# Row sums that are inverted later: raw heads and raw sums leave the attention, and a batched reciprocal and a scaling follow before the output projection

## The reference

```
qkv = x @ w_qkv.T + b_qkv                      # 16 heads of 32
scores = q @ k.T / sqrt(32) + causal mask
attn = softmax(scores); out = attn @ v
x = layernorm(x + out @ w_out.T + b_out)
hidden = relu((x @ sign(up_w).T) * up_scale)   # 2048 wide
x = layernorm(x + (hidden @ sign(down_w).T) * down_scale * output_scale)
```

## Time and profile before

| | us |
|---|---|
| median of 3 runs | 765.48 (764.55 to 766.41) |
| the profiled execution's own time | 763.71 |
| its span in the trace | 761.9 |
| PE busy | 720.6 (95%) |
| DVE busy | 439.5 (58%) |

### The profile page before, as it was taken

How to read it: one execution, slowest core, us unless ns; L and a number is a source line. 1 busy time by engine, 2 the same in 40 slices (tenths; PEclk the granted TensorE clock), 3 DMA queues, 4 the chain that set the end, 5 groups by cost and what they waited for, 6 DMA issues and landing times.

```text
span 761.9 us, 11587 instructions
## 1 busy us (share of the span) xinstructions
PE 720.6 (95%) x4032; PEld 504.0 (66%) x4032; DVE 439.5 (58%) x990; ACT 317.5 (42%) x631; POOL 353.5 (46%) x487
## 2 busy tenths in 40 slices
PE   6899999999999999999989889999999999999993
PEld 4688665665656656565544545887878787878882
DVE  4276495785967859578467652443393349325515
ACT  5211365555656546565456575333222222222210
POOL 4461467394673946739422503632352235223333
PEclk9999999999999999999989999999999999999998
DMA  6976455535555355453577333221012001000101
GB/s 234 310 202 176 107 149 149 144 112 154 150 146 140 109 160 146 124 144 96 154 235 249 103 120 113 69 103 63 1 42 98 28 1 55 3 1 15 41 1 55
DMA packets 44618, 85.70 MB, mean 112 GB/s; under 512 B 4880, under 2 KB 13584, under 8 KB 44432
## 3 DMA queue, kind: packets, MB, share of 16 engines
q1 hardware_dynamic: 35536, 79.72, 34.4%
q10 hardware_dynamic: 9024, 5.24, 2.4%
HBM read 55.33 MB, written 29.36 MB: 111 GB/s over the span
## 4 chain that ended last, share of the span: by engine, by line
PE 74%; DVE 14%; DMA 4%; issue 3%; POOL 2%; ACT 2%; SPq 0%; ACTq 0%; POOLq 0%
PE ps_heads L1039 9%; PE ps_proj L941 8%; PE ps_proj L1081 7%; PE ps_score L1098 6%; PE ps_unit L1081 6%; PE ps_unit L1057 6%; PE ps_sum L1033 5%; PE ps_unit L977 4%; DVE maxes L811 4%; PE ps_unit L1009 4%; DVE heads_sb L830 4%; PE ps_heads L1098 3%; PE ps_sum L1098 3%; PE ps_score L1009 3%; PE ps_score L977 2%
## 5 line engine op out<-in xcount | busy, mean ns | idle before, releaser
L653 POOL TENSOR_TENSOR hid_low<-hid_raw,hid_high 128x512 fp32r<-128x512 f32 x64 | 85.0, 1328 | 174.4 <-DVE hid_high L880 171.3
L709 ACT ACTIVATE probs<-ps_unit 128x512 f32<-128x512 f32 (+3 forms) x216 | 101.9, 490 | 82.6 <-PE ps_unit L1009 80.7
L617 POOL TENSOR_SCALAR_AFFINE_SELECT probs<-probs 128x128 f32<-128x128 f32 x256 | 72.6, 297 | 105.1 <-ACT probs L709 100.6
L709 ACT ACTIVATE probs<-ps_score 128x512 f32<-128x512 f32 (+3 forms) x155 | 75.2, 498 | 74.4 <-PE ps_score L1009 73.0
L880 DVE CAST hid_high<-hid_raw 128x512 fp32r<-128x512 f32 x64 | 27.1, 424 | 125.5 <-ACT hid_raw L764 125.2
L807 DVE CUSTOM_DVE_ANT_0 ps_unit<-ps_unit,causal 128x512 f32<-128x512 f32 (+3 forms) x162 | 80.0, 511 | 32.4 <-PE ps_unit L977 31.8
L977 PE MATMUL ps_unit<-stack 96*128 96x512 f32 (+3 forms) x246 | 83.7, 353 | 5.4 <-DVE maxes L807 2.5
L1039 PE MATMUL ps_heads<-probs,v_rows 128*32 128x512 f32 (+3 forms) x768 | 79.5, 497 | 4.1 <-DVE heads_sb L832 4.1
L1009 PE MATMUL ps_unit<-stack 98*128 98x512 f32 (+2 forms) x216 | 78.7, 367 | 3.3 <-DVE maxes L807 3.2
L611 POOL TENSOR_TENSOR parts<-qk_full,parts 128x512 fp32r<-128x512 f32 x32 | 41.2, 1287 | 64.1 <-ACT parts L688 64.1
L811 DVE TENSOR_REDUCE maxes<-ps_unit 128x1 f32<-128x512 f32 x84 | 55.0, 682 | 19.0 <-PE ps_unit L977 18.9
(11 more groups left out here) (195 smaller groups left out, 1439.3 us busy)
## 6 DMA issues: line engine op xcount, KB each, us to landing
stack<-qk_parts SPq DMA_DIRECT2D x96, 256.0 KB, 4.5
qk_parts<-parts SPq DMA_DIRECT2D x32, 512.0 KB, 3.0
v_all<-h_even ACTq DMA_DIRECT2D x16, 256.0 KB, 3.8
v_rows<-v_all SPq DMA_DIRECT2D x8, 512.0 KB, 4.4
heads_t<-heads_sb SPq DMA_DIRECT2D x16, 256.0 KB, 3.4
raw<-up_w SPq DMA_DIRECT2D x8, 512.0 KB, 4.2
x_tile<-x_rows SPq DMA_DIRECT2D x16, 256.0 KB, 5.1
raw<-down_w SPq DMA_DIRECT2D x8, 512.0 KB, 3.5
```

Source lines behind the costliest of these rows:

```text
L653: nc.gpsimd.tensor_tensor(hid[1][:, (HM * s + n) % 3, :], hid_raw[:, n % 2, :], hid[0][:, (HM * s + n) % 3, :].bitcast(FP32), ALU.subtract ...
L709: nc.scalar.activation(probs[:, (NP * s + n) % RING, 0:width], bank(what, s, n)[:, off:off + width], ACT.Exp, scale=SCALE).then_inc(s_exp, 1)
```

## The change

The job `norm` becomes `copy`: DVE copies `ps_heads` to `heads_sb` and `ps_sum` to a new `sums_sb`, and SP stores both; of the sums it stores one row for each of the 4 heads. All sums of a batch of steps are then loaded as one tile of 128 partitions (`gather`), inverted by DVE (`invert`, L904 in the new file), stored (`scatter`), and spread with a broadcast over 32 partitions into the buffer that later takes the high parts (`spread`, four DMAs of 256 KB for each chunk). A new DVE job `scale` multiplies the loaded heads by it (L909), before ACT and DVE split them. There are four batches: steps 0 to 5; step 6's first half; its second half; step 7. PE's wait before L1039 is now for the copied heads only, and one before L1033 for the copied sums. The table `MAXIMA` is spaced more evenly in its first two thirds.

```
-PAIRED_NORM = [19.73, 52.08]
+PAIRED_COPY = [19.73, 52.08]
-MAXIMA = ([11.5 + 0.5 * u for u in range(3)] + [13.4 + 0.48 * u for u in range(13)]
-          + [26.3 + 0.6 * u for u in range(3)] + [28.4 + 0.53 * u for u in range(14)] + [37.5 + 0.66 * u for u in range(15)])
+MAXIMA = ([11.5 + 0.7 * u for u in range(16)] + [23.4 + 0.73 * u for u in range(17)] + [37.5 + 0.66 * u for u in range(15)])
+BATCHES = [(0, STEPS - 2, 0, 2), (STEPS - 2, STEPS - 1, 0, 1), (STEPS - 2, STEPS - 1, 1, 2), (STEPS - 1, STEPS, 0, 2)]
+COLUMNS = [0, 192, 208, 224, 256]
...
-            put(t + at, "norm", s, q)
-            put(t + at + 4.9, "store", s, q)
+            put(t + at, "copy", s, q)
+            put(t + at + 1.6, "store", s, q)
...
+    for k, at in enumerate((late + 8.5, late + 22.5, last + 6.5, FIRST_UP + 2)):
+        put(at, "gather", k)
+        put(at + (2.9 if k < 3 else 1), "invert", k)
+        put(at + (4.4 if k < 3 else 1.5), "scatter", k)
+    put(late + 28.6, "spread", 0)
+    put(last + 14, "spread", 1)
...
+        put(late + 37 + 2 * i, "scale", 0, i)
         put(late + 38 + 2 * i, "split", 0, i)
+        put(last + 30 + 2 * i, "scale", 1, i)
...
                 put(t - 4, "fetch", i + 1)
+                put(t + 0.2, "spread", i + 1)
...
+                if i:
+                    put(t + 1.7 + 0.7 * q, "scale", i + 1, q)
                 put(t + 2.2 + 0.7 * q, "split", i + 1, q)
...
+                if what == "gather":
+                    _, end, _, f1 = BATCHES[s]
+                    sp.wait_ge(s_sst[0], 16 * end)
+                    sp.wait_ge(s_sst[1], 16 * (end if f1 == 2 else end - 1))
+                    sp.dma_start(columns(s), batch(sums_dram, s)).then_inc(s_gat, 16)
+                if what == "scatter":
+                    sp.wait_ge(s_inv, s + 1)
+                    sp.dma_start(batch(inv_dram, s), columns(s)).then_inc(s_sca, 16)
+                if what == "spread":
+                    f, b = s % 2, s // 2
+                    sp.wait_ge(s_sca, 16 * (2, 3, 4, 4)[s])
...
+                    for h in range(GH):
+                        sp.dma_start(inverses(s)[h * HD:(h + 1) * HD, :, :],
+                                     inv_dram.rearrange("(g b f h q) -> g b f h q", b=2, f=2, h=GH, q=HALF)[:, b, f, h, :]
+                                     .partition_broadcast(HD)).then_inc(s_spr, 16)
...
                 if what == "split":
+                    act.wait_ge(s_nrm, DC * s + n + 1)
...
-                    nc.vector.reciprocal(heads_sb[:, :], ps_sum[:, :]).then_inc(s_rc, 1)
-                    dve.wait_ge(s_rc, 2 * s + n + 1)
-                    nc.vector.tensor_tensor(heads_sb[:, :], ps_heads[:, :], heads_sb[:, :], ALU.mult).then_inc(s_norm, 1)
+                    nc.vector.tensor_copy(heads_sb[:, :], ps_heads[:, :]).then_inc(s_hc, 1)
+                    wait(dve, s_sst[1 - f], 16 * (s + f))
+                    nc.vector.tensor_copy(sums_sb[:, :], ps_sum[:, :]).then_inc(s_norm, 1)
+                if what == "invert":
+                    dve.wait_ge(s_gat, 16 * (s + 1))
+                    nc.vector.reciprocal(columns(s), columns(s)).then_inc(s_inv, 1)
+                if what == "scale":
+                    if n == 0:
+                        dve.wait_ge(s_hl, 16 * (s + 1))
+                        dve.wait_ge(s_spr, 16 * GH * (s + 1))
+                    nc.vector.tensor_tensor(heads_in(s)[:, n, :], heads_in(s)[:, n, :], inverses(s)[:, n, :],
+                                            ALU.mult).then_inc(s_nrm, 1)
```

More of the change, by code:

```diff
@@ L152, in plan @@
             put(t + 43.9, "sum_added", s)
-        for q, at in enumerate(PAIRED_NORM if paired else ALONE_NORM[s % 2]):
-            put(t + at, "norm", s, q)
-            put(t + at + 4.9, "store", s, q)
+        for q, at in enumerate(PAIRED_COPY if paired else ALONE_COPY[s % 2]):
+            put(t + at, "copy", s, q)
+            put(t + at + 1.6, "store", s, q)
         if s + 1 < STEPS:
@@ L262, in build @@
         heads_dram = nc.dram_tensor("heads_t", [GROUPS, P, TOKENS], FP32, kind="Internal").ap()
+        sums_dram = nc.dram_tensor("sums", [STEPS * 2 * GH * HALF], FP32, kind="Internal").ap()
+        inv_dram = nc.dram_tensor("inverses", [STEPS * 2 * GH * HALF], FP32, kind="Internal").ap()
         qk_dram = nc.dram_tensor("qk_parts", [2, NB, P, 2, HALF], FP32, kind="Internal").ap()
@@ L298, in build @@
         s_pv = sem("probs_used")
-        s_rc = sem("row_sum_inverted")
+        s_hc = sem("heads_copied")
+        s_sst = [sem(f"sums_stored{f}") for f in range(2)]
+        s_gat = sem("sums_gathered")
+        s_inv = sem("sums_inverted")
+        s_sca = sem("inverses_stored")
+        s_spr = sem("inverses_spread")
+        s_nrm = sem("heads_scaled")
         s_add = sem("probs_added")
         s_used = sem("added_probs_used")
-        s_norm = sem("heads_normalized")
+        s_norm = sem("heads_and_sums_copied")
         s_st = [sem(f"heads_stored{f}") for f in range(2)]
@@ L346, in build @@
         rstd2 = sb(top, "rstd2", [P, 2], FP32)
+        inv = sb(top, "inv", [P, COLUMNS[-1]], FP32)
         h1_even = sb(top, "h1_even", [P, TT, D], FP32)
@@ L427, in heads_in, with inverses, columns, batch @@
             return heads_raw if s else h1_even
+        def inverses(s):
+            return turned[s % 2][0][:, :, :].bitcast(FP32)
+        def columns(k):
+            return inv[:, COLUMNS[k]:COLUMNS[k + 1]]
+        def batch(dram, k):
+            s0, s1, f0, f1 = BATCHES[k]
+            return dram[(2 * s0 + f0) * GH * HALF:(2 * s1 - 2 + f1) * GH * HALF].rearrange("(p c) -> p c", p=P)
         def bank(what, s, n):
@@ L724, in _ @@
                     else:
+                        if n == 15:
+                            for f in range(2):
+                                act.wait_ge(s_sst[f], 16 * STEPS)
                         if n == 16:
@@ L1022, in _ @@
                     if what == "pv" and j == 0:
-                        wait(pe, s_norm, 2 * s + f)
+                        wait(pe, s_hc, 2 * s + f)
                         if f == 0:
                             pe.wait_ge(s_vl[s % 2], 16 * (s // 2 + 1))
+                    if what == "sum" and j == 0:
+                        wait(pe, s_norm, 2 * s + f)
                     for h in range(GH):
```

19 lines of the change are left out of this document (14 added, 5 removed).

## The result

The changed kernel is slower: 769.50 us median against 764.07 of the kernel before on the same chip, a ratio of 1.0075 (95% interval 1.0057 to 1.0092). In a second session, unchanged (label after_again), it took 767.67 against 763.98, 1.0049 (1.0030 to 1.0068). The profiled execution took 767.28 us with a span of 765.5; before it was 763.71 and 761.9.

The account below looks back on a forecast made before the run. PE was taken to set the time, DVE counting only where PE waits. Terms -10 + 0 + 2.4 - 2.3 + 11.2 = +1.3 us on 763.7 gave 765.0, median 766.8; range 762 to 770 (chance 0.50).

Parts of the forecast that it names:

- Steps 0 to 5: Attention steps: gain of 10 us, 3.6 from heads waits and 6.4 from row maxima; bounds 3.6 and 13.
- signs that the prediction named: Inversion and PE waits with clock 0.50 in step 6; 3.5 us projection waits, clock below 1; no `heads_sb` waits; step 45.5 us.
- Middle of step 6: Reciprocal's 5.7 us stall goes, about 5.7 returns as DVE waits for gathered sums: 0; bounds gain 5.5, loss 2.
- End of step 6: Four `scale` products on DVE, which paces PE there, cost 2.4 us; bounds 0 and 4.5.
- Step 7: Waits for `heads_sb` (0.81 us) and h_even (1.42 us) go: gain of 2.3 us, bounds 0.8 and 4.
- Feed-forward part: PE waits 3.4 us more at each of two chunks, clock falls cost 2.2 each: loss of 11.2 us.
- (2): Rival: POOL stretches the scaling, each chunk waits up to 7.3 us: slower, 776.6 us; chance 0.21 (above 770).
- (1): Rival: gain stays, clock holds in feed-forward and gather lands within 2.2 us: 757.6 us; chance 0.29 together with (3).
- (3): Rival: nothing felt, attention not DVE's and scaling covered, only step 6's 5.7 us goes: 759.8; chance 0.29 with (1).

Follow-up runs that it names:

- e7: Kernel before with its reciprocal of the row sums replaced by a copy, so the division is left out; 765.49 us, ratio 1.0016.
- e6: Changed kernel with the old table MAXIMA of the kernel before; 776.57 us, ratio 1.0157 to the kernel before.
- e5: Kernel before, division as it was, with only the new table MAXIMA of the change; 789.23 us, ratio 1.0340.
- e1: Changed kernel with the load of step 6's first-half sums ahead of the three stack fills in SP's queue; 766.62 us, 1.0039 to the kernel before.
- e9: Kernel before with two more DVE products at each of chunks 2 and 3, half of what the change adds there; 764.94 us, ratio 1.0016.
- e3: Changed kernel with the output projections of chunks 2 and 3 (and their y, ln1, turn) one slot later; 762.81 us, 0.9974 to the kernel before.
- e4: Changed kernel without the eight scalings of chunks 2 and 3, all transfers kept; 759.29 us, ratio 0.9947 to the kernel before.
- e2: Changed kernel with step 6's second inversion six slots later in DVE's order, its store and broadcasts behind it; 772.96 us, 1.0112 to the kernel before.
- e10: e8 with ACT's four up-weight conversions in step 6 one to two slots later and the second inversion one slot later; 760.16 us, 0.9944 to the kernel before.
- e8: Changed kernel with the moves of e1 and e3, and chunk 0's scalings two slots later, spaced 1.8; 756.85 us, 0.9907 to the kernel before.

## Why the prediction was right, and where it was not

The median of 769.50 us is 2.7 above the forecast of 766.8 and 0.5 inside its range of 762 to 770; in the second session it is 0.9 above. The sign of its sum, +1.3 on 763.7, was right: the profile shows +3.6, of which 1.7 are the chance fall at 35 us. The prediction had put slower at 0.42 and faster at 0.41, so it did not claim to know the sign. The steps are less well matched than the sum. Steps 0 to 5 gave 1.7 us less than forecast, step 6 cost 2.1 more, step 7 gave 0.8 less and the chance fall cost 1.7, while the feed-forward part cost 4.0 less than forecast. These errors nearly cancel, and that is luck. Of the signs that the prediction named, the waits in step 6 and at both projections came, and those for `heads_sb` went; the step shrank to 46.0 and not to 45.5 us; and the clock fell at one of the two projections only.

**Steps 0 to 5**, -10 us: measured -8.3, 1.4 a step where I had 1.67. The attribution failed. I gave 0.6 a step to the heads wait and 1.07 to the maxima, as if they were two gains. The reciprocal left out alone gives 0.2 a step (e7), the copies with the old table nothing (e6), and the table without them is a loss of 3.7 a step (e5). With the copies in place the table is the whole gain, 1.4 a step (e6 against the changed kernel). So the old table set the step's pace, and the new one becomes possible only when the reciprocal is gone.

**Middle of step 6**, 0: measured +1.9. PE stood idle 5.48 us instead of my 3; with the clock's 2.1 us (2.82 us of work at 0.50, then 0.83 of 4 us) that is 7.6 against the old 5.7. The mechanism and its cause, the place in the queue behind the stack fills, were right (e1). So was the time of issue: I said 392.5 to 393 on the time of before, and 386.31 with the 6.6 us that step 6 starts earlier is 392.9. The main mis-sized term is the landing, 6.0 us where I took 4. Two smaller ones go the same way: PE ran on for 0.8 us after DVE stopped where I had 1.2, and 0.85 us pass between the landing and PE's next matmul (the inversion and a maximum), which I had left out. Against them DVE came at 386.92, which is 393.5 on the time of before, 1 us later than I had. The bound of a loss of 2 holds the whole.

**End of step 6**, +2.4: measured about +2.3, for another reason. PE's waits from 407 to 422 us grew only from 1.7 to 2.3 us; the clock fell once more (0.80 and 0.77 from 412 to 420), which I estimate at 0.2 and 0.23 of 4 us each, 1.7 us. I had not expected that fall, and had 2.4 of waits instead.

**Step 7**, -2.3: measured -1.5. The wait for the heads went. That for h_even did not go; it fell from 1.42 us to 0.97. The two make 1.3 of the 1.5.

**Feed-forward part**, +11.2: measured +7.2. I had 3.4 us more of waiting at each projection; the waits grew by 3.0 and 2.9, to 3.30 and 3.24. The last split did fall behind POOL's product, which cost 0.85 us where I had 0.7; of the 2.4 us of issue 1.8 show, since one product lies in the first split's own wait (e9). The term that was much too large is the clock: 2.2 us twice, measured once, at 1.7 (0.35 and 0.08 of 4 us each). The upper bound of 7.3 us did not come. The Trainium skill (GPSIMD Engine Reference, Key points) names contention between GpSimd and DVE instructions with two SBUF inputs. The trace agrees in the splits and not in the scalings: no `scale` was stretched (675 and 674 ns on the mean), but the splits were, 1381 and 1449 ns instead of 1234 and 1239.

**The rivals.** (2), scaling stretched by POOL, decides at a mean over 1 us and is out at 0.675. (1), the gain stays, had its point in the clock and in the landing: the landing went against it, and the clock held at one of two places, but behind waits of 3.2 us and not of its 2.5. (3), nothing felt, is refuted by e3 and e4. But what it says of the attention, that its time isn't DVE's reciprocal, e7 bears out.

What stays open: why the clock fell at chunk 3's projection in e1 and not in the changed kernel at a wait of the same length; why the load of the sums took only 3.6 us in e2; where the 1.9 us are by which the medians differ more than the profiled executions; and whether POOL is the better place for chunk 0's scaling.

## What to carry to other kernels

A change that saves work must be read with the order that was fitted to the old work. Leave out the work alone first (e7). If that brings nothing, suspect the order, and try both together; here only both together gained (e5, e6). A division moved behind a round trip through DRAM needs room for four transfers in a queue; look where each stands, since a stall removed at one place uncovers the next (e1, e2, e7, e10). And where PE has no cover for DVE, move PE's own step one place back before shortening DVE's: e3's one slot gave back 6.0 of the 7.2 us, and with the loads in a better order too (e8) the same change is 0.9% faster than before, not 0.5 to 0.75% slower.
